# A LayerNorm and q/k/v projection moved from token-major tiles to feature-major groups of 512 tokens

## What is computed

```python
def _layernorm(x, axis=-1, eps=1e-05):
    m = jnp.mean(x, axis=axis, keepdims=True)
    v = jnp.var(x, axis=axis, keepdims=True)
    return (x - m) / jnp.sqrt(v + eps)
...
    qkv = x @ qkv_w.T + qkv_b                  # x is the normalized input here
    q, k, v = jnp.split(qkv, 3, axis=-1)
...
    q = apply_rope(q)                          # [x1 cos - x2 sin, x1 sin + x2 cos], x1, x2 the halves of a head
    k = apply_rope(k)
    attn = jnp.einsum('bqhd,bkhd->bhqk', q, k) * scale
...
x = x + _L0_attn_ref(_layernorm(x, axis=-1), ...)
x = x + _L0_ffn_ref(_layernorm(x, axis=-1), ...)
```

## Time and profile before

| | us |
|---|---|
| median of 3 runs | 1013.33 (1012.12 to 1013.39) |
| the profiled execution | 1015.13 |
| its span | 1013.2 |
| TensorE busy in the span | 933.0 (92%) |
| VectorE, ScalarE, GpSimd busy | 624.3, 542.7, 305.3 |
| projection, by the timeline | 0 to 143.6 |
| attention | 143.8 to 616 |
| routing and experts | 616 to 1013 |

### The profile page before, as it was taken

How to read it: one execution, slowest core, us unless ns; L and a number is a source line. 1 busy time by engine, 2 the same in 40 slices (tenths; PEclk the granted TensorE clock), 3 DMA queues, 4 the chain that set the end, 5 groups by cost and what they waited for, 6 DMA issues and landing times. The chain is left out here.

```text
span 1013.2 us, 24223 instructions
## 1 busy us (share of the span) xinstructions
PE 933.0 (92%) x6751; PEld 556.3 (55%) x6752; DVE 624.3 (62%) x1360; ACT 542.7 (54%) x1376; POOL 305.3 (30%) x484
## 2 busy tenths in 40 slices
PE   7999945999999999999999988992599999999996
PEld 3566521333333333333333325881599999999996
DVE  5676659888888888888888603676133333333332
ACT  3666630777777778877777882453222222222221
POOL 7566670232233322323223321146011111111111
PEclk9999985899999999999999997996799999999999
DMA  3456553422222211111224206334666565666560
GB/s 107 104 144 170 156 154 115 142 64 65 65 65 63 61 51 51 56 49 51 61 63 147 86 1 232 108 131 157 205 190 207 194 205 196 196 203 201 195 207 24
DMA packets 66729, 125.14 MB, mean 124 GB/s; under 512 B 11506, under 2 KB 44659, under 8 KB 60532
## 3 DMA queue, kind: packets, MB, share of 16 engines
q1 hardware_dynamic: 61092, 102.95, 33.7%
q0 software_dynamic: 5584, 21.54, 5.7%
HBM read 95.96 MB, written 28.48 MB: 123 GB/s over the span
## 5 line engine op out<-in xcount | busy, mean ns | idle before, releaser
L829 ACT ACTIVATE arena<-B_ps_s 128x512 f32<-128x512 f32 (+3 forms) x768 | 327.0, 493 | 127.3 <-PE B_ps_s L966 124.9
L888 DVE TENSOR_REDUCE B_block_max<-B_ps_item 128x8 f32<-128x1024 f32 x288 | 340.7, 1219 | 39.4 <-PE B_ps_item L951 37.5
L966 PE MATMUL B_ps_s<-q_stack,k_stack 99*128 99x512 bf16 (+7 forms) x768 | 190.2, 333 | 3.8 <-ACT arena L829 3.1
L810 POOL TENSOR_SCALAR_AFFINE_SELECT arena<-arena 128x256 f32<-128x256 f32 x256 | 104.2, 408 | 201.1 <-ACT arena L829 198.8
L982 PE MATMUL B_ps_o<-arena,B_v_quad 128*32 128x512 f32 (+3 forms) x1536 | 163.6, 498 | 1.0 <-ACT B_oacc L843 0.7
L966 PEld LDWEIGHTS B_ps_s<-q_stack,k_stack 99*128 99x128 bf16 (+1 forms) x768 | 54.0, 97 | 182.9 <-ACT arena L829 171.9
L1563 PEld LDWEIGHTS D_ps_h<-D_xT,arena 128*128 128x128 f32 x1248 | 146.7, 193 | 4.7 <-ACT D_xT L1501 2.8
L1563 PE MATMUL D_ps_h<-D_xT,arena 128*128 128x128 f32 x1248 | 147.3, 277 | 2.1 <-ACT D_xT L1501 2.1
L1582 PE MATMUL D_ps_y<-arena,D_hr 128*128 x624 | 141.0, 379 | 0.0
L1492 ACT ACTIVATE D_hr<-D_ps_h,ffn_columns 128x128 f32<-128x128 f32 x156 | 44.6, 369 | 164.4 <-PE D_ps_h L1563 164.4
L951 PE MATMUL B_ps_item<-k_stack,q_stack 64*128 64x128 bf16 (+3 forms) x1152 | 111.0, 286 | 21.1 <-DVE B_block_max L888 11.4
(11 more groups left out here) (150 smaller groups left out, 890.1 us busy)
## 6 DMA issues: line engine op xcount, KB each, us to landing
arena<-in_w_exp SPq DMA_DIRECT2D x39, 1024.0 KB
qk_parts<-arena SPq DMA_DIRECT2D x64, 192.0 KB, 2.4
q_stack<-qk_parts SPq DMA_DIRECT2D x96, 128.0 KB, 2.7
rows<-payload SPq DMA_DIRECT2D x39, 257.0 KB, 2.7
k_stack<-qk_parts SPq DMA_DIRECT2D x64, 128.0 KB, 2.7
arena<-in_w_exp POOLq DMA_DIRECT2D x8, 1024.0 KB, 6.7
arena<-in_x SPq DMA_DIRECT2D x32, 128.0 KB, 2.6
k_stack<-qk_parts SPq DMA_DIRECT2D x64, 64.0 KB, 2.3
```

Source lines behind the costliest of these rows:

```text
L810: pool.affine_select(out=block_p, in_=block_p, compare_op=ALU.is_ge, fill=0.0, base=0, pattern=[[0, 2], [1, P]], channel_multiplier=-1).th ...
L829: act.activation(pr[s % PR][:, h, 0:QW - off], ps_s[(QH * s + j) % R][:, 0:QW - off], ACT.Exp, scale=scale).then_inc(s_e, 1)
L888: dve.tensor_reduce(bmx[:, r, g:QH:GH, at:at + 4], src[:, :, :].rearrange("p c (b n) -> p c b n", n=P), AX.X, ALU.max).then_inc(s_free, 1)
L966: pe.matmul(ps_s[(QH * s + j) % R][:, 0:QW - off], ks[rows, r, half, bass.ds(g * SEQ + kb * P, P)], qs[rows, r, half, bass.ds(g * SEQ + c ...
```

## The change

The projection keeps features on partitions throughout. The host hands over x a second time, transposed (`x_feat`, 256 x 4096). The work goes in 8 groups of 512 tokens, each in two halves: h even is q, h odd is k. The mean of LayerNorm is folded into the weights: TensorE multiplies the weights with a matrix of 1/256, VectorE subtracts the column means from them once. The reciprocal deviation of a token is a column of `sd`; four transposes of its broadcast spread it over all partitions of a PSUM bank, and VectorE multiplies x transposed with it. For q and k the weights are now the stationary operand and 512 tokens the columns, so that the output already has features on partitions: the transposes of z and of the rotated tiles are gone, and the bias is ScalarE's per-partition bias as it copies a block of 128 x 512 out of PSUM into `ev`. For the values x transposed is the stationary operand, and ScalarE's copy multiplies with the token's scale.

The order of features puts the lower halves of all 16 heads in one block of 128 and the upper halves in the other. VectorE makes two products of 1024 elements, `ev` x cosines and `ev` x sines, from SBUF to SBUF; GpSimd subtracts and adds, 512 elements each. The three parts follow as before, on 1024 elements, from SBUF. A half is stored with two stores of 384 KB in runs of 1 KB. `qk_parts` has another order of its axes; stack loads still read rows of 4 KB. Everything is emitted without a loop. The second stack is loaded in the projection (steps 10 to 13) instead of at the start of attention. The rotation table grows from 256 KB to 1 MB. The split of the q/k bias is gone. The order of the loads at the start is x (512 KB), weights (768), constants (64), x transposed (512), bias (2), x, the table, and the rest.

```diff
-        xt = early(DIM)
-        z = early(DIM)
-        zt = early(DC * P).rearrange("p r (c n) -> p r c n", c=DC)
...
+        xt = take("early", XR, TG * DIM).rearrange("p r (t n) -> p r t n", t=TG)
+        xf = take("early", XR, DC * QW).rearrange("p r (c n) -> p r c n", c=DC)
...
+        ps_qk = [ps(f"ps_qk{i}", [P, 2, QW]) for i in range(2)]
+        ps_v = ps("ps_v", [P, 2, DIM])
+        ps_bc = ps("ps_scale", [P, QW])
...
+                for h in range(NH + 2):                                   # SP
+                    if h % 2 == 0:
+                        load_x(h // 2 + XR)
+                    if h >= 2:
+                        store(h - 2)
+                    if h % 2 == 1:
+                        load_features(h // 2 + XR)
+                    if h == 6:
+                        for g in range(2):
+                            sp.wait_ge(s_st[g], 64)
+                    if 6 <= h < 10:
+                        load_stack(sp, Step(0), qs, ks, parts_d, s_stk, range(4 * (h - 6), 4 * (h - 5)))
+                    if 10 <= h < 14:
+                        load_stack(sp, Step(1), qs, ks, parts_d, s_stk, range(4 * (h - 10), 4 * (h - 9)))
...
+                for h in range(NH + 2):                                   # ScalarE
+                    m = h - 1
+                    if h < NH:
+                        for c in range(2):
+                            act.wait_ge(s_qk, 2 * h + c + 1)
+                            if h >= 2:
+                                act.wait_ge(s_pd, h - 1)
+                            act.activation(ev[:, h % 2, c, :], ps_qk[h % 2][:, c, :], ACT.Identity,
+                                           bias=bq[:, 2 * (h % 2) + c:2 * (h % 2) + c + 1]).then_inc(s_ev, 1)
+                    if 0 <= m < NH:
+                        act.wait_ge(s_rot, 2 * (m + 1))
+                        if m >= 4:
+                            act.wait_ge(s_st[m // 2 - 2], 64)
+                        act.activation(parts(m, 0), rot[:, m % 2, :, :], ACT.Copy).then_inc(s_p1, 1)
+                    if m >= 1:
+                        act.wait_ge(s_r1, m)
+                        act.activation(parts(m - 1, 1), res[:, (m - 1) % 2, :, :], ACT.Copy).then_inc(s_p2, 1)
+                    if h < NH:
+                        for t in (2 * h, 2 * h + 1):
+                            value(t)
+                    if h % 2 == 1:
+                        root(h // 2 + 2)
...
+                def normalize(g):                                         # VectorE
+                        dve.tensor_tensor(z[:, g % 2, :, :], xf[:, g % XR, :, :],
+                                          ps_bc[:, :].unsqueeze(1).to_broadcast([P, DC, QW]), ALU.mult).then_inc(s_z, 1)
...
+                for h in range(NH + 1):
+                    m = h - 1
+                    if h < NH:
+                        if h % 2 == 0:
+                            inverse(h // 2 + 1)
+                        dve.wait_ge(s_ev, 2 * (h + 1))
+                        if h >= 2:
+                            dve.wait_ge(s_r1, h - 1)
+                        for out, table, done in ((rot, 0, s_pc), (ds, 1, s_pd)):
+                            dve.tensor_tensor(out[:, h % 2, :, :], ev[:, h % 2, :, :],
+                                              rp[:, table, positions(h)].unsqueeze(1).to_broadcast([P, 2, QW]), ALU.mult).then_inc(done, 1)
+                    if m >= 0:
+                        dve.wait_ge(s_p1, m + 1)
+                        if m >= 2:
+                            dve.wait_ge(s_p3, m - 1)
+                        dve.tensor_tensor(res[:, m % 2, :, :], rot[:, m % 2, :, :], parts(m, 0), ALU.subtract).then_inc(s_r1, 1)
+                    if h < NH and h % 2 == 0:
+                        normalize(h // 2 + 1)
+                    if h < NH:
+                        t = 2 * h + 2 * TG
+                        for u in range(2):
+                            stats(t + u)
+                        variances(t, t + 2)
...
+                for h in range(NH + 2):                                   # GpSimd
+                    m = h - 2
+                    if h < NH:
+                        pool.wait_ge(s_pc, h + 1)
+                        pool.wait_ge(s_pd, h + 1)
+                        for c, op in ((0, ALU.subtract), (1, ALU.add)):
+                            pool.tensor_tensor(rot[:, h % 2, c, :], rot[:, h % 2, c, :], ds[:, h % 2, 1 - c, :], op).then_inc(s_rot, 1)
+                    if m >= 0:
+                        pool.wait_ge(s_p2, m + 1)
+                        pool.tensor_tensor(parts(m, 2), res[:, m % 2, :, :], parts(m, 1), ALU.subtract).then_inc(s_p3, 1)
...
+                for h in range(NH):                                       # TensorE
+                    g = h // 2
+                    pe.wait_ge(s_z, g + 1)
+                    for c in range(2):
+                        if h >= 2:
+                            pe.wait_ge(s_ev, 2 * (h - 2) + c + 1)
+                        at = (2 * (h % 2) + c) * P
+                        for k in range(DC):
+                            mm = pe.matmul(ps_qk[h % 2][:, c, :], wq[:, k, at:at + P], z[:, g % 2, k, :], start=(k == 0), stop=(k == DC - 1))
+                        mm.then_inc(s_qk, 1)
+                    if h == 0:
+                        pe.wait_ge(s_wc, 3)
+                    values(2 * h, 2 * h + 2)
+                    if h % 2 == 0:
+                        spread(g + 1)
...
                 for s in s_st:                                            # attention, SP
-                    sp.wait_ge(s, 64 * (NT // len(s_st)))
-                load(Step(1))
+                    sp.wait_ge(s, 64)
```

More of the change, by code:

```diff
@@ L438, in _, with root, value @@
-                steps(act, emit)
+                def root(g):
+                    if g < NG:
+                        act.wait_ge(s_var, TG * (g + 1))
+                        act.activation(sd[:, g % 4, 0, :], mv[:, g % 2, :, 1], ACT.Sqrt, bias=eps).then_inc(s_sd, 1)
+                def value(t):
+                    g = t // TG
+                    act.wait_ge(s_mv, t - t % 2 + 2)
+                    act.wait_ge(s_rs, g + 1)
+                    act.activation(v_all[:, t, :], ps_v[:, t % 2, :], ACT.Copy, scale=sd[:, g % 4, 1, t % TG:t % TG + 1]).then_inc(s_v, 1)
@@ new lines, in variances, with inverse @@
+                def variances(first, last):
+                    for t in range(first, last):
+                        g, i = t // TG, t % TG
+                        if g < NG:
+                            dve.wait_ge(s_bn, t + 1)
+                            dve.bn_aggr(mv[:, g % 2, i, :], st[:, g % 2, i, :]).then_inc(s_var, 1)
+                def inverse(g):
+                    if g < NG:
+                        dve.wait_ge(s_sd, g + 1)
+                        dve.reciprocal(sd[:, g % 4, 1, :], sd[:, g % 4, 0, :]).then_inc(s_rs, 1)
@@ L519, in _ @@
+                add_value_bias(dve, ps_v[:, 0, :])
             @block.gpsimd
@@ L597, in _, with spread, values @@
-                steps(pe, emit)
+                def spread(g):
+                    if g < NG:
+                        pe.wait_ge(s_rs, g + 1)
+                        pe.wait_ge(s_z, g)
+                        for t in range(TG):
+                            mm = pe.transpose(ps_bc[:, t * P:(t + 1) * P], sd[:, g % 4, 1, t:t + 1].to_broadcast([P, P]), ident)
+                        mm.then_inc(s_bc, 1)
+                def values(first, last):
+                    for t in range(first, last):
+                        g, i = t // TG, t % TG
+                        if t % 2 == 0 and t >= 2:
+                            pe.wait_ge(s_v, t)
+                        if i == 0:
+                            pe.wait_ge(s_xf[g % XR], 16 * (g // XR + 1))
+                        for c in range(DC):
+                            mm = pe.matmul(ps_v[:, t % 2, :], xf[:, g % XR, c, i * P:(i + 1) * P], wq[:, c, 2 * DIM:3 * DIM],
+                                           start=(c == 0), stop=(c == DC - 1))
+                        mm.then_inc(s_mv, 1)
@@ new lines, in _ @@
+                pe.wait_ge(s_one, 1)
+                pe.wait_ge(s_wl, 16)
+                for k in range(3):
+                    dst = ps_v[:, 0, :] if k == 2 else ps_qk[0][:, k, 0:DIM]
+                    for c in range(DC):
+                        mm = pe.matmul(dst, mean[:, :], wq[:, c, k * DIM:(k + 1) * DIM], start=(c == 0), stop=(c == DC - 1))
+                    mm.then_inc(s_wm, 1)
+                pe.wait_ge(s_cst, 16)
+                spread(0)
+                pe.wait_ge(s_wc, 2)
```

385 lines of the change are left out of this document (124 added, 261 removed).

## The result

| | before | after |
|---|---|---|
| median (range), us | 1013.36 (1012.12 to 1015.87, 4 runs) | 1037.36 (1026.06 to 1040.75, 4 runs) |
| ratio, 95% interval | | 1.0214 [1.0129, 1.0299] |
| profiled execution, us (span) | 1015.13 (1013.2) | 1040.32 (1038.4) |
| mask cast starts (attention begins) | 143.87 | 145.76 |
| C_lt cast starts (attention is over) | 615.36 | 638.49 |

The change is 2.1% slower, 24 us by the medians. The forecast was 1027 with 1018 to 1040, so number and sign look right. The table says that the reason is not: of the 25.2 us between the spans, 1.9 lie in the projection, where 13.6 were forecast, and 21.2 in the attention, of which the prediction said that it does not change. That the number fell into the range is luck.

A forecast was written before the change was run, and what follows sets the result against it. TensorE was taken to bound the projection, VectorE the attention's opening, TensorE the rest. The projection would end 14.6 us later, less 1.0 from fewer stores: 1013.3 + 13.6 = 1027 us, range 1018 to 1040.

The forecast's parts named there:

- TensorE is relieved, the bound moves to VectorE and GpSimd: Projection: TensorE falls to 5.65 us a half, while VectorE and GpSimd together need 8.3.
- The pair excludes each other: Projection: VectorE instructions with two SBUF inputs and GpSimd instructions reading SBUF cannot overlap, 3.3 and 4.86 us a half.
- 8.16 us a half: Projection: VectorE's 3.3 us and GpSimd's 4.86 us one after the other in each half.
- 8.3: Projection: us a half for VectorE and GpSimd, 8.16 plus 0.06 at some three changes of side; 16 halves make 133.
- 3.3 net: Projection: us a half of VectorE's two products and one subtraction, 1.10 each after a wait, instead of 3.75.
- 4.86: Projection: us a half of GpSimd, two rotation instructions at 1.27 each and the third part at 2.32.
- three handovers of 0.06: Projection: 0.06 us added at some three changes of side between VectorE and GpSimd in each half.
- evacuated at 21.3: Projection's start: first q/k matmul at about 15.8 us, half 0 takes 4.7 to 20.5, copied out of PSUM at 21.3.
- The attention and all after it don't change: Everything behind the projection: no difference in time, 0 us.
- The second stack's load costs nothing where it stands now: Stack load moved from attention's opening into the projection: its 14 issues, 8.1 us uncovered, stand between stores; opening stays 33 us.
- The sum: Projection 14.6 us later, less 1.0 us from fewer stores: 13.6 us, so 1027 for the whole kernel.
- the rivals: Whole kernel: no lock (8%, 988 us), one-sided wait (5%, 998), the clock falls (7%, 1042), idle pair (8%, 1043).

The follow-up runs named there:

- Run 5: The changed kernel with VectorE's two products taken straight from PSUM and ScalarE's copies of the banks gone: 1010.24 us, ratio 0.9951.
- run 1: The changed kernel with 150 more TensorE instructions (75 tiny matmuls and their weight loads) behind the projection: 1020.28 us, ratio 1.0092.
- run 8: The kernel of run 1 with 134 waits on an already set semaphore at the start of ScalarE's stream: 1014.29 us, ratio 1.0031.
- run 7: The kernel of run 1 with 67 waits on an already set semaphore at the start of ScalarE's stream: 1021.89 us, ratio 1.0069.
- run 2: The kernel before with 160 more TensorE instructions (80 tiny matmuls, 40 ahead of and 40 behind its projection work): 1035.81 us, ratio 1.0231.
- run 3: The changed kernel with 256 more TensorE instructions (128 tiny matmuls) behind the projection: 1035.32 us, ratio 1.0187.
- run 9: The kernel of run 1 with 180 waits on an already set semaphore at the start of ScalarE's stream: 1025.36 us, ratio 1.0136.

## Why the prediction was right, and where it was not

- **TensorE is relieved, the bound moves to VectorE and GpSimd**: right. TensorE is busy 84.36 of 116 us, 73% (65 to 70 forecast; the halves are shorter, and its granted clock is 0.92 on the mean of this stretch). ScalarE's durations were within 5% (evacuation 0.68, copies 1.06 and 1.04, values 0.46 us).
- **The pair excludes each other**: right, on both sides, also the side for which before had no row. The Trainium skill, page SBUF — State Buffer, section Who interferes with whom, has this rule: whichever starts first holds the port for its whole length. The trace agrees: every large pair on the timeline above ends one after the other. Run 5 takes one side's second SBUF input away from the products, and 23.3 us of the projection go.
- **"8.16 us a half", "8.3"**: too long; it is 7.8 for the half on the timeline and 7.7 on the mean. VectorE's 3.3 net is measured as 3.35. GpSimd's 4.86 is 4.45: its instructions too had begun while they waited, so that behind the wait 1.12 of the 1.27 us were left, which I had netted off on VectorE alone; and the third part takes 2.10, not 2.32. The three handovers of 0.06 don't exist. From the first product to the last GpSimd part 134.7 us were forecast, 125.7 measured: 9.0 less, about sixteen times the difference between 8.3 and 7.7.
- **"evacuated at 21.3"**: the first product starts at 18.68, 2.6 us sooner. The weights were there at 6.47 us instead of 8.2, and the q/k matmuls of half 0 took 3.67 us instead of 4.7, at a granted clock of 1.00. 9.0 and 2.6 together are the 11.6 by which the last part ends before 156.0, at 144.40. (The 1218 KB of the start count three x tiles in all, not three behind the first; the rate of 220 KB a us is right.)
- **"The attention and all after it don't change"**: this step failed, and it is where the time is. What the attention's loop computes didn't change; where its code lies did. Of the 21.2 us, TensorE's fetches make 15.8 (492.7 to 476.9 by run 1) and ScalarE's 5.9 (to 471.0 by run 8), which is 0.5 below the 471.5 of the kernel before. The shares hold in this order only: run 5, with TensorE's fetches and none of ScalarE's, takes 490.9, so beside TensorE's stalls ScalarE's show for 2 us.
- **The second stack's load costs nothing where it stands now, and the attention's opening keeps its length**: right, first exponentials 182.21 against 180.31 with a start 1.9 us later.
- **The sum**: 13.6 forecast for the projection, 1.9 found; 0 forecast for the attention, 21.2 found. With both loops resident the change is worth +0.31% [0.19, 0.43], 3 us, by run 8. The forecast number lies between the changed kernel with both loops fetched and with both resident, and describes neither: it was in range because two errors, 11.7 us too much for the projection and 21.2 too little for the attention, partly cancel. None of the rivals had the mechanism.
- **Not explained**: the last stage, 397.9 to 399.9 us, 2.0 longer. It takes 395.0 to 400.8 in the eleven profiled executions, with no order in it by the edits (395.0 in run 8, 400.8 in run 7), so the 2.0 need not come from the change. Nor is it known why the changed kernel's own runs spread from 1026 to 1041 and those of run 5 from 997 to 1014, where the resident kernels keep within 0.4%. Runs 2 and 3, with fetches on q8 too, spread by 0.6%.

A reading, not shown by itself: a pass of 6.6 blocks touches 7 or 8 blocks depending on where it begins, and ScalarE's 339 recorded instructions, 2.6 blocks of 128, touch 3 or 4; the loop would stay where the smaller number is touched. The packets of a fetched pass fit: nine on q8 (after, runs 2, 3 and 5) and five on q14 (run 1), one more than the larger number, as if a block behind the loop's end were fetched ahead. All nine runs fit, but the block borders were not located. The Trainium skill, page Runtime: NRT & Kernel Launch, section Instruction fetch mechanics, says that a taken branch whose target isn't in the window of instructions at hand waits for a fetch. The stalls at the returns are of that kind, 2.6 to 4.2 us each. The same section puts that window at two blocks, by which every return of this loop would stall; the trace of before, with 6.6 blocks and no fetch, doesn't agree.

## What to carry to other kernels

An edit ahead of a hardware loop can change the loop's time through nothing but its instruction count, here the attention's by 1 to 5%. When a stage that wasn't touched gets slower, compare the instruction queues of the two kernels within it before looking for a cause in the data, and before judging the edit repeat it with the count shifted by half a block (here 75 tiny matmuls in idle time): here it is the difference between +2.1% and +0.9% (+0.3% with ScalarE's loop moved too), and between 0.9951 and 0.9809. And count the SBUF inputs of VectorE's instructions that run beside GpSimd: moving one operand back to PSUM was worth 23 us.

## What the runs showed of the hardware that was not expected

- TensorE's loop of some 1,690 instructions runs 250 us without an instruction fetch, or fetches nine blocks of 16 KB in every pass, by its place: 0 and 256 instructions more are alike, 150 or 160 more turn it round, in either kernel. Fetching makes a pass 3 to 8 us longer (85.8 to 87.7 against 83.0 of run 1; 85.8 to 89.7 in run 2 against 81.2 to 81.5): an idle stretch of 2.6 to 4.2 us at the return (4.2 in run 5), and behind it, at all but one of the returns (run 2's first), the granted clock at 0.50 for 3.4 to 6.8 us.
- ScalarE's loop does the same with blocks of 8 KB on the other queue, for 1.8 us a pass in run 1 (83.0 against 81.2) and 3.7 in run 9 (85.0); of the four places tried, 0, 33, 67 and 91 recorded instructions on, only the third is good.
- GpSimd's tensor_tensor waits for a running VectorE instruction with two SBUF inputs as VectorE waits for it: 1.27 us became up to 2.29, and some 0.15 us of an instruction's length are hidden in the wait on either side.
